# Turning the routed rows of a two-layer adapter kernel: 32x32 blocks on VectorE in place of four TensorE transposes a round

## The reference, cut to what matters

```python
# layer 0: mix channels by a chosen 64x64 matrix, then base weight + routed low-rank experts
y = einsum('bct,bcd->bdt', x, weights[condition])
result = y @ W_base.T + b_base
probs = softmax(y @ W_gate.T); top_p, top_i = top_k(probs, 2); top_p /= sum(top_p)
route_w = sum(one_hot(top_i, 8) * top_p)
hw = (y @ A.T) * route_w              # 8 experts x rank 16 = 128 columns: "routed rows"
x = x + result + hw @ B
# layer 1: a 1024x1024 matrix per sample, then scored low-rank experts
z = x @ w[adapter_id].T
scores = 8 * softmax(z @ Wr.T + br)
x = x + 2 * ((z @ A1.T) * scores) @ B1     # "scored rows"
```

## Time and profile before

| | us |
|---|---|
| median of 3 runs | 733.42 (732.48 to 733.96) |
| the profiled execution's own time | 733.35 |
| its span, first to last instruction | 731.7 |
| TensorE busy in it | 719.5 (98%) |
| VectorE busy | 340.0 (46%) |
| ScalarE busy | 113.7 (16%) |

### The profile page before, as it was taken

The page is one execution under the profiler, slowest core; times in us unless marked ns, Lnnn a source line. Parts: engine busy times, 40 slices in busy tenths (PEclk is TensorE's granted clock), DMA queues, the critical chain, the costliest instruction groups (busy, mean ns, idle before and its releaser), DMA issues.

```text
span 731.7 us, 12347 instructions
## 1 busy us (share of the span) xinstructions
PE 719.5 (98%) x4502; PEld 646.1 (88%) x4502; DVE 340.0 (46%) x887; ACT 113.7 (16%) x309; POOL 57.9 (8%) x115
## 2 busy tenths in 40 slices
PE   8899999999999999999999999999999999999996
PEld 8899998898889988898889888988889888998996
DVE  2000196056625544465426561654346543684644
ACT  2122310031103110022003100311012100320111
POOL 1122410001100000001000110001000100010100
PEclk9999999999999999999999999999999999999999
DMA  7799993506754467248714674447733782386552
GB/s 285 290 416 377 367 411 102 213 4 197 244 196 174 141 232 283 99 133 295 277 78 177 227 241 189 180 134 240 266 110 138 266 299 85 147 311 227 203 212 73
DMA packets 38848, 156.23 MB, mean 214 GB/s; under 512 B 8852, under 2 KB 11924, under 8 KB 28564
## 3 DMA queue, kind: packets, MB, share of 16 engines
q1 hardware_dynamic: 27858, 78.72, 28.5%
q0 software_dynamic: 9216, 71.31, 28.3%
q10 hardware_dynamic: 1730, 5.58, 1.9%
HBM read 133.24 MB, written 22.35 MB: 213 GB/s over the span
## 4 chain that ended last, share of the span: by engine, by line
PE 94%; SPq 2%; DMA 2%; DVE 1%; issue 1%; ACT 0%; POOLq 0%; DVEq 0%
PE base_ps L344 18%; PE base_ps L345 18%; PE base_ps L346 18%; PE base_ps L358 8%; PE out_ps L418 4%; PE low_ps L418 4%; PE mix_both L372 4%; PE mix_both L383 3%; PE out_ps L372 2%; PE low_ps L372 2%; PE out_ps L344 2%; PE out_ps L345 2%; PE out_ps L346 2%; PE out_ps L383 2%; PE low_ps L383 2%; PE mix_both L385 1%
## 5 line engine op out<-in xcount | busy, mean ns | idle before, releaser
L344 PE MATMUL base_ps<-yT,w_hi 128*128 128x512 f32 (+1 forms) x576 | 213.5, 371 | 1.3 <-DVE xT L815 1.1
L346 PE MATMUL base_ps<-yT,w_hi 128*128 128x512 f32 (+1 forms) x576 | 211.6, 367 | 0.0
L345 PE MATMUL base_ps<-yT,w_lo 128*128 128x512 f32 (+1 forms) x576 | 211.4, 367 | 0.0
L344 PEld LDWEIGHTS base_ps<-yT,w_hi 128*128 128x128 f32 x576 | 108.5, 188 | 21.2 <-DVE xT L815 4.0
L346 PEld LDWEIGHTS base_ps<-yT,w_hi 128*128 128x128 f32 x576 | 108.4, 188 | 17.9
L345 PEld LDWEIGHTS base_ps<-yT,w_lo 128*128 128x128 f32 x576 | 108.5, 188 | 16.0
L854 DVE TENSOR_TENSOR xT<-xT,out_ps 128x512 f32<-128x512 f32 (+1 forms) x53 | 35.3, 667 | 102.8 <-PE out_ps L346 102.8
L358 PE MATMUL base_ps<-ag_raw,stage 128*128 128x136 f32 x640 | 76.7, 283 | 2.0 <-DMA stage<-in_w 2.0
L358 PEld LDWEIGHTS base_ps<-ag_raw,stage 128*128 128x128 f32 x640 | 76.3, 194 | 2.4 <-issue 2.2
L966 POOL DMA_DIRECT2D adapter<-folded x60 | 31.9, 532 | 561.3 <-PE low_ps L418 488.3
L711 DVE TENSOR_TENSOR x1T<-xT,x1T 128x256 fp32r<-128x256 f32 x120 | 45.3, 420 | 59.7 <-ACT x1T L585 59.6
(11 more groups left out here) (158 smaller groups left out, 843.8 us busy)
## 6 DMA issues: line engine op xcount, KB each, us to landing
adapter<-folded POOLq DMA_DIRECT2D x63, 1088.0 KB, 5.4
stage<-in_w SPq DMA_DIRECT2D x39, 512.0 KB, 7.4
x_rows<-in_x SPq DMA_DIRECT2D x32, 512.0 KB, 8.8
xT<-in_x_turned SPq DMA_DIRECT2D x16, 1024.0 KB, 6.3
out<-xT SPq DMA_DIRECT2D x28, 512.0 KB, 2.7
folded<-adapter ACTq DMA_DIRECT2D x10, 544.0 KB, 6.8
w_raw<-in_w SPq DMA_DIRECT2D x8, 256.0 KB, 8.4
w_raw<-in_w SPq DMA_DIRECT2D x4, 512.0 KB, 12.6
```

Of the source, the lines that this page charges most:

```text
L344: pe.matmul(dst, st_hi, mv_lo, start=start, stop=False, skip_group_check=True)
L345: pe.matmul(dst, st_lo, mv_hi, start=False, stop=False, skip_group_check=True)
L346: return pe.matmul(dst, st_hi, mv_hi, start=False, stop=stop, skip_group_check=True)
```

## The change

The four TensorE transposes of `turn_hw` go. VectorE turns the same rows in 32x32 blocks, from `rows` into the part of `hg` that held the unrouted columns (free once `rows` is written): 16 instructions a round in four groups of four, one group for each 32 tokens of all four tiles, each instruction 32 partitions by 4x32 elements. `hwT_done` now counts four groups. In rounds with layer 1 the groups stand behind `sum_low(2)`, `sum_low(3)`, `sum_low(4)` and `sum_low(5)`; in round 0 they stand behind `routing`, and round 0's `hwT_low` moves to behind the first split of the right half. ScalarE's copy and VectorE's subtraction read `hg` in SBUF in place of PSUM. `turn_lw` and the tail's turn stay as they were.

```diff
+        hw_turned = hg[:, :, 0:HR]
+        BLOCK = 32
+        def by_tile(columns):
+            return columns.rearrange("p (t n) -> p t n", n=P)
# TensorE
-            def turn_hw(q, r):
-                pe.wait_ge(route_step, at(q, r, ROUTE_STEPS, ROUTE_STEPS))
-                for t in range(TILES):
-                    mm = pe.transpose(mix_ps[0][:, t * P:(t + 1) * P], rows[:, t, :], identity[:, :])
-                mm.then_inc(hwT_done, 1)
-                    if k == 5:
-                        turn_hw(q, r)
# ScalarE
-                act.wait_ge(hwT_done, at(q, r, 1, 1))
-                act.copy(hwT[:, 0, :], mix_ps[0][:, :]).then_inc(hwT_hi_done, 1)
+                act.wait_ge(hwT_done, at(q, r, P // BLOCK, P // BLOCK))
+                act.copy(by_tile(hwT[:, 0, :]), hw_turned).then_inc(hwT_hi_done, 1)
# VectorE
+            def turn_hw(q, r, n):
+                if n == 0:
+                    dve.wait_ge(route_step, at(q, r, ROUTE_STEPS, ROUTE_STEPS))
+                tok = n * BLOCK
+                for rank in range(0, P, BLOCK):
+                    block_turned = dve.transpose(hw_turned[rank:rank + BLOCK, :, tok:tok + BLOCK],
+                                                 rows[tok:tok + BLOCK, :, rank:rank + BLOCK])
+                block_turned.then_inc(hwT_done, 1)
             def hwT_low(q, r):
                 dve.wait_ge(hwT_hi_done, at(q, r, 1, 1))
-                dve.tensor_tensor(hwT[:, 1, :], mix_ps[0][:, :], hwT[:, 0, :], ALU.subtract).then_inc(hwT_lo_done, 1)
+                dve.tensor_tensor(by_tile(hwT[:, 1, :]), hw_turned, by_tile(hwT[:, 0, :]), ALU.subtract
+                                  ).then_inc(hwT_lo_done, 1)
                     for i in range(2, PER):
                         x1T_low(q, r - 1, i)
                         sum_low(q, r - 1, i - 2)
-                hwT_low(q, r)
-                if l1:
+                        if i >= 4:
+                            turn_hw(q, r, i - 4)
+                    hwT_low(q, r)
                     sum_low(q, r - 1, PER - 2)
# VectorE, ahead of round 0's iteration
             routing(0, 0)
+            for n in range(P // BLOCK):
+                turn_hw(0, 0, n)
             for k in range(0, KC, 2):
                 split(w_hi[:, k:k + 2, T:D], w_lo[:, k:k + 2, T:D], w_raw[:, k:k + 2, T:D], w_landed[KC + k // 2],
                       HALF1 + k // 2)
+                if k == 0:
+                    hwT_low(0, 0)
```

## The result

The changed kernel is slower: 736.02 us median (733.36 to 737.07, 7 runs) against 733.51 for the kernel before in the same comparison, a ratio of 1.0035 with a 95% interval of 1.0019 to 1.0051. The forecast was 731.0. The profiled execution of the changed kernel took 734.6 us, with a span of 732.9.

A forecast was written before the change was run, and what follows sets the result against it. TensorE, busy for 98% of the span, was taken as the bound: -2.64 (rounds 1 to 6) - 0.46 (round 0) + 0.79 (last round) = -2.31 us from 733.35, so 731.0 us; range 729.8 to 733.7.

The forecast's parts named there:

- T: Time a group of four block transposes takes from VectorE; forecast 0.9 us, against 0.82 at the elementwise rate.
- successive transposes don't overlap: Rival on VectorE's transposes: T = 1.14, last round +1.75, round 0 nothing, 732.0 us, no change; chance 0.12.
- -3.10 + 2.31 + 0.48: Sum: gross gain 3.10 us on TensorE, last round's cost 4T - 2.81, round 0's cost 4(T - 1.16).
- the estimate of 1.24 for a group: T if four VectorE transposes run in line at the skill's 311 ns each for 128x128 in bf16.
- The 0.8 to 0.95 of the other estimate: T by the skill's section 3.8: transpose array pipelined to sustain one element per cycle per lane.
- Rounds 1 to 6 ... Cost: none: Groups fit VectorE's 1.74 us idle gaps in rounds 1 to 6; cover 1.4 us, gone from T = 1.9.
- the last rival: VectorE becomes the bound: T = 1.7, last round +3.99, round 0 +2.16, 736.4 us; chance 0.08.
- Removed work: Four TensorE transposes a round gone: 0.44 us in each of rounds 1 to 6, 0.46 in round 0, last round nothing.
- 4T - 2.81: Last round's cost from VectorE's late chain, nothing below T = 0.70; 0.79 us at T = 0.9.
- The wait for `add_base` was to become 1.9: Sign in the last round: TensorE's wait for VectorE's `add_base` grows from 1.1 to some 1.9 us.
- no wait for `hwT` anywhere: Sign: TensorE never waits for the turned rows; in the last round `hwT` complete at 658.9, ahead of 659.18.
- -0.46 + 0.48: Round 0: TensorE gains 0.46 us; VectorE's groups cost nothing up to T = 1.16, then 4(T - 1.16).

The follow-up runs named there:

- e10: The changed kernel with a plain copy in place of each block transpose, so rows are not turned: 732.75 us, ratio 0.9991 to the kernel before.
- e2: The changed kernel with VectorE turning in rounds 1 to 6 only, TensorE in round 0 and the last: 731.37 us, ratio 0.9975 to the kernel before.
- e5: e2 with 16 one-column memsets ahead of all other VectorE work: 732.26 us, ratio 0.9982 to the kernel before.
- e3: The changed kernel with VectorE's loop over rounds 1 to 6 written out as straight code: 734.19 us, ratio 1.0012 to the kernel before.
- e8: The kernel before with VectorE's loop written out: 733.93 us, ratio 1.0010 to the kernel before.
- e6: VectorE turns the rows in the last round only, TensorE in rounds 0 to 6 as before: 736.99 us, ratio 1.0057 to the kernel before.
- e1: The changed kernel once more, unedited: 735.87 us, ratio 1.0034 to the kernel before.
- e7: The changed kernel with 6 and 12 throwaway TensorE transposes in the last round's waits: 733.63 us, ratio 1.0007 to the kernel before.
- e9: The kernel before with 19 throwaway TensorE transposes ahead of the last half round, 2.1 us later: 735.75 us, ratio 1.0039 to the kernel before.
- e4: The changed kernel with VectorE turning in rounds 1 to 6 only and its loop written out: 730.50 us, ratio 0.9968 to the kernel before.

## Why the prediction was wrong

**The first step that failed** is the price: "I take T = 0.9: nearest to the elementwise row, plus 20 ns an instruction". T was 1.28. I had taken the spacing of two large independent subtractions (0.34 us for a duration of 0.42) as the overlap that any two instructions have. The block transposes don't overlap at all, and neither do copies of this shape (e10). The mechanism was among the rivals, "successive transposes don't overlap", with T = 1.14 from the durations and a chance of 0.12; by my own sum a T of 1.28 gives -3.10 + 2.31 + 0.48 = -0.31, that is 733.0 and no change. The Trainium skill ("VectorE: DVE Perf Modes", "The three transpose paths") gives 311 ns for a 128x128 turn in bf16; the 302 ns here, for the same 128 elements a partition but in fp32 and on 32 partitions, lie close to it. I had the estimate of 1.24 for a group, worked out from it, in the text and weighed it too lightly. The 0.8 to 0.95 of the other estimate did not come out.

This step explains 2.15 of the 4.8 us by which the forecast's change was missed (last round 2.14 in place of 0.79, round 0 +0.34 in place of -0.46). It alone would have left the time inside the range. What put it outside are two costs that the prediction set at nothing: "Rounds 1 to 6 ... Cost: none", and waits of TensorE priced by their length, with no effect on its clock. That the result lies near the last rival's 736.4 is chance: that rival asks for T = 1.7.

**Removed work: right, where it could be seen.** Rounds 1, 2, 4 and 6 became 0.44 to 0.48 us shorter against 0.44 forecast. In the last round the transfers took it back in the trace after (1.37 us of waits for them in place of 0.74, so 0.63 more against 0.44 forecast).

**Rounds 1 to 6 cost nothing: wrong for two of them.** No view of before hints at it: the added instructions cost 0.5 us at each jump back, because of what stands ahead of the loop body (e2 without, e5 with, e3 and e8 as controls). Size 0.9 to 1.0 us.

**The last round: mechanism right, size off.** 4T - 2.81 gives 2.31 for T = 1.28; 2.14 was measured, and 2.16 in e6. The wait for `add_base` was to become 1.9 and became 2.04; "no wait for `hwT` anywhere" failed (0.89 us), as it had to from T = 0.97.

**Round 0: size off.** -0.46 + 0.48 was due with the true T; +0.34 was measured. TensorE's wait for `add_base` is listed with 0.55 us, counted from the end of the matmul before it:

```profile
124.14 0.39 PE L353 MATMUL base_ps<-hwT,b_hi 128*128 128x512 f32 x1
125.08 0.47 PE L351 MATMUL base_ps<-yT,w_hi 128*128 128x512 f32 x1 [0.55 <-DVE xT L825]
```

By starts, the measure that the prediction uses for the turns, it costs 0.94 - 0.23 = 0.71 us, and the next start comes 0.08 late as well: 0.79 - 0.46 = 0.33.

**What was in no case: the clock.** The prediction ended its account at TensorE's waits, priced by their length. They can cost more: in e1 a half-clock stretch beside them took another 1.36 us, in e10 one took 1.46. e7, with the waits filled, was 2.0 to 2.2 us faster than the changed kernel at the same work of VectorE; how much of it belongs to this place and how much to the tail is not shown. The tail is long in all five traces in which VectorE turned the last round's rows (after, e1, e3, e6, e7: 17.1 to 17.2 us), in e10's with copies there (16.96) and in e9's (16.99). In the other five (before, e2, e4, e5, e8) it is 15.8. e9 shows that a shift in time alone can do it, and the times since the clock's first rise (under e9) part the twelve traces without exception. So the tail's 1.35 us in the pair before and after is in part luck: most of the 2.2 us by which the tail came later after that rise (710.4 in place of 708.1) lies ahead of round 0, where nothing was changed. Whether the last round's waits act on the tail in another way as well, over 55 us, is not settled.

**Why slower at all.** Per execution: 0.67 us before the tail (round 0 +0.34; rounds 1, 2, 4 and 6 together -1.86; rounds 3 and 5 together -0.02; the last round +2.14 and +0.07), 1.35 in the tail, and in part of the executions 1.36 beside the last round's waits. That makes 2.0 to 3.4; the medians differ by 2.4 to 2.5. Only -0.25 us of it, the part before the tail without the stall's 0.9, could have been worked out from the profile of before. The range ended at 733.7 since it took the slow prices singly and no loss outside VectorE's price.

## What to carry to other kernels

Price an instruction of a shape that the trace doesn't have by a full duration, with no overlap, until a row of the same shape shows one: here 32-partition blocks had none, and 128x32 instructions in the same trace start 0.11 us apart at a duration of 0.19. When work goes to an engine with "room", find the one round where it has none: here the last round lost 2.14 us and more with the clock, nearly all that rounds 1 to 6 can give (2.6). Leaving it and round 0 to TensorE (e2, e4) turned a loss of 0.35% into a gain of 0.25 to 0.32%. Instructions in a looped stream, and even ahead of it, can cost at the jump back; the count of instruction packets, and one that falls into the gap, show it. Before a difference in a late stretch is put down to a change, look where the clock fell in both traces: the same mean can hide it.

## What the runs showed of the hardware

- A block transpose on VectorE, fp32, 32 partitions by 128 elements, takes 302 ns and starts 0.32 us after its like; a copy of the same operands 218 ns and 0.23 (after, e10). Two-operand instructions of 128x32 start 0.11 us apart at 0.19 us each (before).
- With 16 more instructions ahead of VectorE's loop of two rounds, the trace shows 22 instruction packets against 12 and 1.5 us more of idle time for VectorE at each jump, of which TensorE saw 0.5. An instruction packet of 8 KB begins in the gap (after: 307.67 and 464.81 us). That VectorE waits for it is read from the times; the view doesn't name its engine.
- The granted clock fell to its half level (1.2 of 2.4 GHz) in the middle of a busy program, amid waits of TensorE of 0.27, 0.68, 1.34 and 1.00 us within 10 us (e1), in some executions and not in others (the first trace after had 1.03, 0.34, 0.89 and 2.04 us of waits there and kept its clock). It cost 1.4 us, and 1.5 in e10. With eighteen throwaway transposes in the waits the mean clock was 0.999 or 1.000 in seven of twelve runs, against one of e1's eight, and the median 2.0 to 2.2 us lower, on another chip.
- In the tail, the same sequence of matmuls and waits ran at the full clock or at the half clock depending on when it came (e9, 2.1 us later: 1.2 us longer).
- The stretch up to round 0's `mix`, the same in all twelve traces, took 85.0 to 85.5 us without and 85.8 to 88.5 us with a half-clock stretch in it.
